# Issuing the routed experts' weight loads from ScalarE's queue instead of SyncE's, in a one-core attention, gated-scan and mixture-of-experts kernel

## The reference, cut to what matters

```python
def _expert(x, wg, wu, wd):
    return jax.nn.silu(x @ wg) * (x @ wu) @ wd
...
shared_out = _expert(x, shared_gate, shared_up, shared_down)
logits = x @ Wr * routing_bias
probs = jax.nn.sigmoid(logits)
scores, idx = jax.lax.top_k(probs, TOPK)
...
for e in range(n_exp):
    combined = combined + _expert(xf, routed_gate[e], routed_up[e], routed_down[e]) * weights[:, e:e + 1]
return shared_out + combined.reshape(b, s, d)
```

## Time and profile before

| | |
|---|---|
| median of 3 runs | 2221.99 us (2218.77 to 2223.56) |
| the profiled execution, its time | 2221.99 us |
| its span, first to last instruction | 2220.2 us |
| mean granted TensorE clock | 0.892 of full |
| busy over the span: PE / DVE / ACT / POOL | 80% / 67% / 49% / 34% |

### The profile page before, as it was taken

How to read it: one execution, slowest core, us unless ns; L and a number is a source line. 1 busy time by engine, 2 the same in 40 slices (tenths; PEclk the granted TensorE clock), 3 DMA queues, 4 the chain that set the end, 5 groups by cost and what they waited for, 6 DMA issues and landing times.

```text
span 2220.2 us, 51528 instructions
## 1 busy us (share of the span) xinstructions
PE 1784.6 (80%) x19596; PEld 1323.1 (60%) x19596; DVE 1486.9 (67%) x2914; ACT 1096.7 (49%) x2670; POOL 747.6 (34%) x850
## 2 busy tenths in 40 slices
PE   2777777777777787787777787756599999999997
PEld 1454555555555555555555555534487888888886
DVE  1687777877778778777877787756474444444447
ACT  1555655665556556655665556543264333333332
POOL 2344243424333434243424333312802333333320
PEclk8888888888988888888889888867799999999999
DMA  2200000000000000010000000003151111111143
GB/s 84 67 17 17 17 25 24 17 17 27 22 17 17 28 21 17 17 32 17 17 17 26 23 17 17 6 4 95 58 153 59 43 49 49 42 47 49 45 165 111
DMA packets 64092, 88.35 MB, mean 40 GB/s; under 512 B 9489, under 2 KB 52129, under 8 KB 63857
## 3 DMA queue, kind: packets, MB, share of 16 engines
q1 hardware_dynamic: 53104, 51.89, 7.8%
q0 software_dynamic: 10752, 33.17, 4.3%
HBM read 66.68 MB, written 18.35 MB: 38 GB/s over the span
## 4 chain that ended last, share of the span: by engine, by line
PE 45%; DVE 15%; issue 6%; ACT 4%; POOL 3%; DMA 0%; DVEq 0%; SPq 0%; ACTq 0%; POOLq 0%
PE ps L1052 15%; PE ps L743 7%; PE ps L1079 7%; PE ps L751 5%; PE ps L738 5%; POOL experts L688 3%; DVE experts L1452 2%; DVE experts L1462 1%; PE ps L1043 1%; DVE work L1434 1%; ACT experts L1200 1%; ACT work L1160 1%; DVE experts L1478 1%; PE ps L1084 1%; DVE experts L1512 1%
## 5 line engine op out<-in xcount | busy, mean ns | idle before, releaser
L1052 PE MATMUL ps<-work,experts 128*128 128x256 f16 x3564 | 406.7, 275 | 16.4 <-ACT work L1365 3.9
L1052 PEld LDWEIGHTS ps<-work,experts 128*128 (+1 forms) x3564 | 346.1, 99 | 64.6 <-issue 6.2
L738 PE MATMUL ps<-cst,experts 128*128 128x128 f32 x1376 | 238.4, 313 | 124.3 <-DVE experts L1512 56.7
L1160 ACT ACTIVATE experts<-ps 128x512 f16<-128x512 f32 (+3 forms) x416 | 253.3, 647 | 80.2 <-PE ps L738 73.6
L743 PE MATMUL ps<-experts 128*128 128x512 f32 (+1 forms) x640 | 284.1, 585 | 1.4 <-ACT experts L1160 1.4
L738 PEld LDWEIGHTS ps<-cst,experts 128*128 128x128 f32 x1376 | 178.3, 160 | 174.6 <-issue 111.4
L1160 ACT ACTIVATE work<-work 128x768 f16<-128x768 f32 x108 | 91.1, 843 | 367.5 <-PE ps L1084 234.8
L1219 ACT ACTIVATE experts<-ps,experts 128x256 f32<-128x256 f32 x512 | 235.2, 475 | 64.2 <-DVE experts L1452 64.2
L617 POOL TENSOR_TENSOR experts<-experts,cst 128x128 f32<-128x128 f32 x256 | 135.0, 564 | 287.5 <-DVE experts L1462 287.5
L1160 ACT ACTIVATE work<-ps 128x128 f32<-128x128 f32 (+3 forms) x214 | 109.9, 514 | 200.3 <-PE ps L738 198.4
L1079 PE MATMUL ps<-experts,work 128*128 (+1 forms) x1620 | 196.7, 274 | 3.7 <-DVE work L1737 3.7
(11 more groups left out here) (192 smaller groups left out, 3135.5 us busy)
## 6 DMA issues: line engine op xcount, KB each, us to landing
experts<-in_ctx SPq DMA_DIRECT2D x32, 512.0 KB, 4.5
experts<-choice_out POOLq DMA_DIRECT2D x8, 1024.0 KB, 13.7
experts<-in_x SPq DMA_DIRECT2D x32, 128.0 KB, 2.2
token_in<-experts SPq DMA_DIRECT2D x32, 128.0 KB, 1.7
work<-token_in SPq DMA_DIRECT2D x32, 128.0 KB, 2.8
work<-in_L_ffn_routed_gate SPq DMA_DIRECT2D x8, 352.0 KB, 3.1
work<-in_L_ffn_routed_up SPq DMA_DIRECT2D x8, 320.0 KB, 4.3
out<-x_all POOLq DMA_DIRECT2D x5, 512.0 KB, 3.3
```

Source lines behind the costliest of these rows:

```text
L738: ins = pe.transpose(bank[:, k * P:(k + 1) * P], a, ident)
L1052: ins = pe.matmul(out, experts_h[:, e, lo:lo + P], e_rows_t[k][:, b * DK + kk, :], start=(kk == 0 and a + b == 0), stop=(kk == DK - 1 and ...
L1160: nc.scalar.activation(dst, src, ACT.Copy).then_inc(done, 1)
```

## The change

The weight loads of the routed experts move from SyncE's queue to ScalarE's. SyncE keeps the bias, the tiles' rows and the stores. On ScalarE the first five chunks are issued after `rows_copy(0, 0)`, behind a wait for VectorE's clearing of `e_hid`, and before the first `silu`. Each later load stands right before the `chunk_high(n)` of its turn n, with the wait for `chunk_lo_ready` that it had.

```diff
 # SyncE
-        def load_chunk(n):
-            wait(sp, S["chunk_lo_ready"], CHUNK_AFTER[n] + 1)
-            if CHUNK_PLACE[n] >= 5:
-                sp.wait_ge(S["table_ready"], 1)
...
-        def load_chunks(t):
-            for n in chunks_of(t):
-                for m in range(5, NCHUNK * NE):
-                    if max(m - 4, CHUNK_AFTER[m] + 1) == n:
-                        load_chunk(m)
         sp.dma_start(r_bias, rbias.partition_broadcast(P)).then_inc(S["consts_loaded"], 16)
-        load_rows(0, 0)
-        for n in range(5):
-            load_chunk(n)
         for t in range(FIRST):
-            if t + 1 < FIRST:
-                load_rows(t + 1, t + 1)
-            load_chunks(t)
+            load_rows(t, t)
 # ScalarE
+        def load_chunk(n):
+            wait(act, S["chunk_lo_ready"], CHUNK_AFTER[n] + 1)
+            if CHUNK_PLACE[n] >= 5:
+                act.wait_ge(S["table_ready"], 1)
+            e, c = n // NCHUNK, n % NCHUNK
+            raw, done = w_raw[CHUNK_PLACE[n]], chunk_loaded[CHUNK_SEM[n]]
+            if c < DK:
+                act.dma_start(raw[:, 0:HID], rgate[e, c * P:(c + 1) * P, :]).then_inc(done, 16)
+                act.dma_start(raw[:, HID:HID + HR], rup[e, c * P:(c + 1) * P, HID - HR:]).then_inc(done, 16)
+                act.dma_start(raw[:, HID + HR:2 * HID], rup[e, c * P:(c + 1) * P, 0:HID - HR]).then_inc(done, 16)
...
         def chunks(t, part):
             for n in part_of(chunks_of(t), part):
+                for m in range(5, NCHUNK * NE):
+                    if max(m - 4, CHUNK_AFTER[m] + 1) == n:
+                        load_chunk(m)
                 chunk_high(n)
...
         rows_copy(0, 0)
+        act.wait_ge(S["cleared"], 2)
+        for n in range(5):
+            load_chunk(n)
         tile(0, 0, True)
```

More of the change, by code:

```diff
@@ L1373, in hidden_high @@
             copy(e_hid_s[0][:, c, :].rearrange("p c n -> p (c n)"), e_hid, S["hid_hi_ready"])
+        def load_chunk(n):
[8 more added lines that the diff above has]
+                act.dma_start(raw[:, HID + HR:2 * HID], rup[e, c * P:(c + 1) * P, 0:HID - HR]).then_inc(done, 16)
+            else:
+                k = HT // 2
+                lo, hi = (c - DK) * k * P, min((c - DK + 1) * k * P, HID)
+                full = (hi - lo) // P
+                act.dma_start(raw[:, 0:full * D].rearrange("p (c n) -> p c n", n=D),
+                              rdown[e, lo:lo + full * P, :].rearrange("(c p) n -> p c n", p=P)).then_inc(done, 16)
+                if full < k:
+                    for at in (0, HR):
+                        act.dma_start(raw[at:at + HR, full * D:k * D], rdown[e, lo + full * P:hi, :])\
+                            .then_inc(done, 16)
         def chunk_high(n):
```

## The result

The changed kernel takes 2244.39 us (median of 4 runs, 2237.24 to 2245.24) against 2221.89 us before in the same rounds. The ratio is 1.0091, 95% interval 1.0075 to 1.0107: slower by 17 to 24 us. The forecast was 2238 us, with 2227 to 2249 as its range. Over all 21 recorded executions of the changed kernel the median is 2241.67 us, about 20 us above before's, so the 22.5 us between the two medians of four are at the upper side. One recorded execution (2649.07 us at a mean granted clock of 0.705, with the loads behind the high parts) was in a slower state and counts in no ratio.

A forecast was written before the change was run, and what follows sets the result against it. It took the bound to be VectorE's routing, GpSimd's tables, then TensorE's own tile work. Head 1.6, tiles 4 to 9 12.7 and clock 2.0 make 16.3 us on 2221.99: 2238 us, range 2227 to 2249.

The forecast's parts named there:

- The head: Before the first `silu`: 13 issues on ScalarE make `hidden(0, 0)`, VectorE's routing and GpSimd's tables late, 1.6 us taken.
- the three cases: `hidden(0, 0)` late by 2.5 us without overlap, 1.5 if issues overlap `rows_copy`, 0.3 if the table load goes first too.
- SyncE's freed queue: 70 DMA issues leave SyncE and tiles' rows no longer stand behind chunk loads: worth 0.
- Tiles 1 to 3: Some 11 us longer together, inside the cover, at least 19 us in which TensorE waits for GpSimd anyway: cost 0.
- Tiles 4 to 9: 43 issues and their waits in ScalarE's queue delay `silu(t, 1)`, or chunk 27 in tile 9, stalling TensorE: 12.7 us taken.
- with and without overlap: Whether a DMA issue can go on while ScalarE's previous ACTIVATE runs; tiles 4 to 9 sum to 11.3 with, 14.0 without.
- The clock: TensorE's granted clock falls after stalls: 1.5 us for tile 7, 0.5 for tiles 4, 8 and 5; sum 2.0, ends 0 and 5.
- The free issue: Rival: issues cost ScalarE nothing and only the waits stay, 2223.6 to 2224.1 us; chance 0.11.
- The dear issue: Rival: an issue on ScalarE costs as much as GpSimd's 0.94 us, up to 2266 us; chance 0.07.
- GpSimd's stretch: GpSimd's one-hot tables, 59.05 us on the chain, slower per instruction beside a busy VectorE; forecast unchanged in length.
- the faster rival: VectorE's work moves out of GpSimd's stretch and its instructions speed up, 2217 us if all 36.76 us move; chance 0.03.
- a changed length: Sign of being wrong: GpSimd's 59 us run, forecast unchanged, changes its length.

The follow-up runs named there:

- the loads behind the high parts: Changed kernel with the first five chunks back on SyncE and later loads behind their part's high parts or `silu(t, 1)`: 2223.09 us, ratio 1.0008.
- the waits alone: Kernel before, with ScalarE given only the waits in front of each `chunk_high`, SyncE still issuing every load: 2223.24 us, ratio 1.0009.
- SyncE's DMAs are cut: Kernel before, with each large gate and up DMA cut in two of half the bytes, issued from SyncE: 2224.65 us, ratio 1.0007.
- the head alone: Changed kernel with only the first five chunks (13 DMAs) issued by ScalarE, all later loads on SyncE: 2223.55 us, ratio 1.0013.

## Why the prediction was right, point by point

*The head.* 1.6 us was taken, between 0.3 and 2.5; `hidden(0, 0)` came 1.44 us later, and GpSimd 1.42. Of the three cases the middle one is true: issues overlap `rows_copy`, the table load doesn't overtake them. What the head step missed is the rows of tile 1. I put SyncE's freed queue at 0. TensorE waited 1.38 us for these rows in the profile before, 3.23 us in that of the waits alone, where GpSimd started 30.92 us after the store of tokens in place of 29.36, and 3.59 us where SyncE's DMAs are cut (31.68). After the change it didn't wait, nor in the other three profiles with the head on ScalarE. So where these rows land late, the change may give back up to about what the head costs: GpSimd's start at 30.92 us in that one profile is no earlier than the 30.78 after the change. By the head alone's ratio it isn't so in the typical execution.

*Tiles 1 to 3* cost nothing, as said; 17.5 of 24.3 us of the cover are left. VectorE's work in GpSimd's stretch ends 8.3 us later (48.36 in place of 40.05), less than the 11 us forecast.

*Tiles 4 to 9.* Added stall, forecast with and without overlap, and measured (idle before the next gate, less that of before):

| tile | forecast | measured |
|---|---|---|
| 4 | 1.8 to 2.0 | 2.28 |
| 5 | 0.6 to 1.3 | 1.43 |
| 6 | 0.3 to 1.3 | 0.65 |
| 7 | 4.3 to 4.8 | 4.42 |
| 8 | 2.5 to 2.6 | 2.57 |
| 9 | 1.8 to 2.0 | 1.97 |
| sum | 11.3 to 14.0, 12.7 taken | 13.3 |

The way of working is what held: start from what TensorE wants next, find the instruction it waits for, and add up what now stands in front of that on its own queue, the waits included.

*The clock.* This term was mis-sized, 2.0 us with 5 as its upper end. In the profile it is 2.23 + 1.67 + 1.57 = 5.5 us (gates of tiles 8, 9 and 10 against 4.09, 4.09 and 5.39), above that end. I priced the one stall longer than those of the rows at 1.5, stalls of 2 to 2.6 us at 0.5 together, and tile 9's at 0, since its drop was "there already"; it cost 1.57 more behind 5.57 us of idleness than behind 3.60. The runs show that stalls of 2 to 3 us often pay too: 1.7 us after 2.90 and 2.19 us, none after 2.28 us. Whether a stall lowers the clock differs between executions, which may be a part of why the median lies 10 us above the profiled execution; another is the loop over pairs, which was 4.9 us shorter in this execution than in the one before and near the shortest of all profiles. How the 10 us divide isn't shown.

*The rivals.* The free issue is out: an issue took about 0.45 us on ScalarE's queue, and 16 more in tiles 4 to 9 cost 8.4 us of stalls. The dear issue is out by the same number. The Trainium skill, "DMA: Bandwidth & Descriptors", "Issuing engines are not separate DMA queues", says that DMAs from several engines run on the same DMA engines, and that the sequencer's time saved is usually small beside the transfer. The trace agrees with the second: 0.45 us an issue against 3.42 us from the last issue of chunk 27 to its landing (3.46 from SyncE). But small did not mean free, since with the waits this time stood in series with the chain. GpSimd's stretch: 48 instructions in 48.36 us, with VectorE busy for 36.97 of them, and 17 in 9.68 us beside an idle one. VectorE's busy time in it is the same as before (36.76), only spread out, and the stretch changed by 1 us; the faster rival did not come at its size. The 1 us itself doesn't look like chance: GpSimd's 64 tables took 58.0 to 58.6 us in the five profiles in which ScalarE's waits spread VectorE's work over tiles 1 to 3, and 59.0 to 59.5 us in the five others. The prediction had named a changed length as a sign of being wrong; it had counted on none.

*The sum.* 1.4 + 13.3 + 5.5 - 1.0 (GpSimd) is 19.2 us and the stage grew by 18.9; the median moved by 22.5, interval 17 to 24. Against the 16.3 us forecast, head and stalls came within 0.6 us each, so the number was not met by errors that cancel: the clock term, 3.5 us too small, is nearly the whole difference.

## What to carry to other kernels

A DMA issue and its wait on a computing engine's queue cost what stands behind them. Find the instruction on that queue that the bounding engine waits for, and put issues behind it or where the engine idles anyway. Here the same issues with the same waits cost 22 us in front of it and some 2 us behind it. Look for a wait that breaks a pipeline of two engines: "load n + 4 waits for the low part of n - 1" was harmless on an idle queue and made ScalarE and VectorE take turns on this one. Alone that cost about 3 us of stalls; with the issues in the same chain it was 13. And look at a stall of the multiplying engine twice: the idle time, and the slower work that may follow (here 13.3 and 5.5 us).

## What the runs showed of the hardware

ScalarE's sequencer issues DMAs while an earlier ACTIVATE still runs (both start at 1512.94 us). An issue of the gate-and-up loads beside tiles 4 to 9 took it 0.33 to 0.48 us, SyncE 0.33 to 0.43 and one 0.58. The 13 of the head took 7.28 us together (SyncE 7.47). The table load placed behind them started at 1520.25, when all 13 were issued. TensorE's granted clock after idle times of 2.1 to 2.9 us is not settled by their length: 36 matmuls took 4.09 us after 2.28 us, and 5.76 us after 2.19 us of idleness, in two kernels with the same work there. GpSimd took 1.25 us for a table beside a busy VectorE and 0.57 us beside an idle one (17 in 9.68 us).
